# One-hot rows of slot positions: made tile by tile by POOL in place of two halves by DVE

## What is computed

```python
xn = _layernorm(x)
# spiking attention: every projection is normalised and compared with a threshold
Q, K, V = (lif(layer_norm(xn @ W.T + b, g, beta), 1.0) for each of q, k, v)   # zeros and ones
attn = Dh - hamming(Q, K) + log_pe_bias(N, N)       # 16 heads of 16
out = lif(einsum(attn * scale, V), 0.5)
s = lif(layer_norm(out @ Wo.T + bo, go, betao), 1.0)
# feed-forward with 8 experts: each token goes to the nearest centroid
xr = _rms_norm(xn, scale)
ids = argmin(_dist2(xr, centroids))
a, g = split(xr @ up_w[ids]); y = (a * silu(g)) @ down_w[ids]
return x + s * _silu(y + xn)
```

## Time and profile before

| | us |
|---|---|
| median of 3 runs | 417.1 (416.22 to 418.41) |
| the profiled execution's own time | 416.2 |
| its span, first to last instruction | 414.4 |

### The profile page before, as it was taken

One profiled execution on the slowest core, in us unless ns is written; L12 is line 12 of the kernel. 1 busy time (PEld: TensorE's weight loads), 2 busy tenths in 40 slices (PEclk: granted clock), 3 DMA queues, 4 the chain that ended last, 5 costly groups with the idle time before them and its releaser, 6 DMA issues.

```text
span 414.4 us, 10171 instructions
## 1 busy us (share of the span) xinstructions
PE 377.2 (91%) x2661; PEld 315.4 (76%) x2662; DVE 323.3 (78%) x829; ACT 227.6 (55%) x606; POOL 225.3 (54%) x330
## 2 busy tenths in 40 slices
PE   3686999999996889899899999999999999999991
PEld 3665877877785678778678888888888888888881
DVE  4965788898866998987857777787778777778873
ACT  1464778788777033353545555555555555555551
POOL 1245678778773011225744666666666666666642
PEclk9978999999998999999989999999999999999998
DMA  5458466695652021222841222222323223232000
GB/s 192 153 153 254 143 191 177 190 291 149 162 153 76 2 78 30 76 88 68 249 148 43 85 85 67 70 84 86 97 60 93 82 80 89 87 93 67 26 15 0
DMA packets 31649, 44.86 MB, mean 108 GB/s; under 512 B 4041, under 2 KB 25714, under 8 KB 31492
## 3 DMA queue, kind: packets, MB, share of 16 engines
q1 hardware_dynamic: 25040, 29.38, 23.9%
q0 software_dynamic: 6240, 14.71, 12.2%
q10 hardware_dynamic: 340, 0.42, 0.3%
HBM read 36.28 MB, written 15.61 MB: 125 GB/s over the span
## 4 chain that ended last, share of the span: by engine, by line
PE 36%; DMA 19%; DVE 16%; issue 10%; POOL 9%; ACT 5%; POOLq 2%; DVEq 1%; SPq 1%; ACTq 0%
PE bank L556 10%; DMA row_a<-rows_a,slot_id 10%; PE bank L574 10%; DMA xs<-in_x 7%; PE bank L399 4%; ACT d_hi L734 3%; PE bank L445 3%; DMA rows_a<-xn 3%; DVE d_lo L1077 2%; PE bank L528 2%; POOL sq L1165 2%; DVE e_hl L1080 2%; POOL inv_std L1140 2%; DVE up_lo L1035 2%; PE bank L539 2%
## 5 line engine op out<-in xcount | busy, mean ns | idle before, releaser
L1077 DVE TENSOR_TENSOR d_lo<-down_sb,d_hi 128x1024 fp32r<-128x1024 f32 x39 | 47.8, 1225 | 34.2 <-ACT d_hi L734 34.2
L1202 POOL DMA_INDIRECT row_a<-rows_a,slot_id x39 | 41.2, 1057 | 47.1 <-DVE e_o L1091 46.1
L734 ACT ACTIVATE d_hi<-down_sb 128x1024 fp32r x39 | 41.4, 1061 | 45.0 <-PE bank L574 38.8
L1235 POOL DMA_INDIRECT out_x<-e_o,slot_id x39 | 44.0, 1129 | 20.8 <-issue 14.5
L556 PE MATMUL bank<-up_hi,e_xh 128*128 x156 | 52.4, 417 | 0.7 <-ACT e_xh L716 0.7
L556 PE MATMUL bank<-up_hi,e_xl 128*128 x156 | 49.2, 397 | 1.2 <-DVE e_xl L1055 1.2
L556 PE MATMUL bank<-up_lo,e_xh 128*128 x156 | 48.9, 395 | 0.0
L1208 POOL DMA_INDIRECT row_s<-rows_s,slot_id x39 | 39.6, 1017 | 15.8 <-issue 11.6
L399 PE MATMUL bank<-w_hi,x_hi 128*128 128x264 f32 (+1 forms) x128 | 42.5, 414 | 0.8 <-DVE dots L883 0.8
L662 ACT ACTIVATE junk<-bank 128x256 bf16<-128x256 f32 x96 | 36.0, 379 | 9.5 <-PE bank L403 8.4
L685 ACT ACTIVATE junk<-bank 128x256 bf16<-128x256 f32 x32 | 12.0, 383 | 46.9 <-PE bank L479 46.9
(11 more groups left out here) (209 smaller groups left out, 1021.7 us busy)
## 6 DMA issues: line engine op xcount, KB each, us to landing
up_raw<-in_up_w SPq DMA_DIRECT2D x16, 512.0 KB, 5.1
rows_a<-xn SPq DMA_DIRECT2D x32, 128.5 KB, 2.8
xs<-in_x SPq DMA_DIRECT2D x8, 512.0 KB, 3.6
rows_a<-in_x SPq DMA_DIRECT2D x8, 512.0 KB, 6.4
down_sb<-in_down_w SPq DMA_DIRECT2D x8, 512.0 KB, 5.1
rows_s<-s_out SPq DMA_DIRECT2D x8, 256.0 KB, 2.5
blk_tab<-in_blocks SPq DMA_DIRECT2D x1, 1024.0 KB, 5.7
row_a<-rows_a,slot_id POOLq DMA_INDIRECT x39, 3.4
```

The source lines that it names most:

```text
L734: act.activation(d_hi[:, :, :], down_sb[:, bass.ds(e, 1), :, :].rearrange("p a c n -> p (a c) n"), ACT.Copy).then_inc(d_high, 1)
L1077: V.tensor_tensor(d_lo[:, :, :], down_sb[:, bass.ds(e, 1), :, :].rearrange("p a c n -> p (a c) n"), d_hi[:, :, :].bitcast(F32), ALU.subtra ...
L1202: G.indirect_dma_start(row_a[s % 4][:, :], None, rows_a, bass.IndirectOffsetOnAxis(ap=slot_id[:, s:s + 1], axis=0), bounds_check=N - 1, oo ...
L1235: G.indirect_dma_start(out, bass.IndirectOffsetOnAxis(ap=slot_id[:, s:s + 1], axis=0), e_o[s % 4][:, :], None, bounds_check=N - 1, oob_is_ ...
```

## The change

`low_hot` is no longer made by DVE. POOL makes it with one `tensor_scalar` per tile, 16 in each half: the row of column numbers `col_no` (128x128, f32) is compared with one column of `rt[:, 1]` as a scalar per partition. The 16 for q = 0 stand behind `norms_out(0)`, the 16 for q = 1 behind `norms_out(1)`. DVE raises a new semaphore `low_made` behind the instruction that writes `rt[:, 1]`; POOL waits for it ahead of `norms_out(0)`, as it does now for the other conditions of the buffers. POOL raises `low_hots` behind each half, and PE waits for it, besides for `slot_hot`, ahead of the 16 matmuls of that half.

```diff
             for q in range(2):
                 pe.wait_ge(slot_hot, q + 1)
+                pe.wait_ge(low_hots, q + 1)
                 for n in range(HT):
                     last = pe.matmul(bank[6][:, 0:2 * ST], low_hot[q][:, n, :],
...
             step(V.scalar_tensor_tensor(rt[:, 1, :], rt[:, 0, :], -float(P), rt[:, 2, :], ALU.mult, ALU.add))
+            dve.sem_inc(low_made, 1)
...
-                if q == 0:
-                    dve.wait_ge(xt_done, NT)
-                    for k in range(4):
-                        dve.wait_ge(row_put[k], 16 * NT // 4)
-                V.tensor_tensor(low_hot[q][:, :, :], over_s(col_no[:, :], P), per_t(rt[:, 1, ts], P), ALU.is_equal)
                 step(V.tensor_tensor(high_hot[:, :, :], over_s(tile_no[:, :], ST), per_t(rt[:, 0, ts], ST), ALU.is_equal))
...
+            def low_one_hots(q):
+
+                for n in range(HT):
+                    last = G.tensor_scalar(low_hot[q][:, n, :], col_no[:, :], rt[:, 1, q * HT + n:q * HT + n + 1], None,
+                                           ALU.is_equal)
+                last.then_inc(low_hots, 1)
+
+            pool.wait_ge(low_made, 1)
+            pool.wait_ge(tables_made, 6)
+            pool.wait_ge(xt_done, NT)
+            for k in range(4):
+                pool.wait_ge(row_put[k], 16 * NT // 4)
             for c in range(NCH):
                 norms_out(c % 2, c // 2)
+                if c < 2:
+                    low_one_hots(c)
```

More of the change, by code:

```diff
@@ L244, in build @@
             sem("hot_done"), sem("ranks_done"), sem("pos_done"), sem("slot_hot"), sem("slots_summed"), sem("slots_made"))
+        low_made, low_hots = sem("low_made"), sem("low_hots")
         m_done, cvec_done, sv_done = sem("m_done"), sem("cvec_done"), sem("sv_done")
```

## The result

The changed kernel takes 426.6 us (median of 4 runs, 423.2 to 428.4) against 417.4 of the kernel before in the same rounds: a ratio of 1.023, with a 95% interval of 1.018 to 1.028. Timed again twice, it gave 1.026 (1.021 to 1.032) and 1.028 (1.024 to 1.033). By the medians of the three comparisons it is 9 to 11 us slower, where 2.1 were forecast and 5.9 were the end of the range. Now and then an execution of one and the same kernel takes over 1.5% longer than its fastest one: the ratios in this document leave such executions out, the medians and spans hold them, unless one is named as left out.

What follows compares the result with a forecast made beforehand. Bound: a chain of waits through all engines, lastly DVE, to PE's `attend(4)`. POOL's sixteen comparisons (5.3 us per half), holds of 2.0 and 4.5 and 0.13 for the semaphore make `attend(4)` 2.1 us late: 417.1 + 2.1 = 419.2 us, range 415.9 to 423.0.

Steps and rivals of the forecast that it cites:

- The saving on DVE: Ahead of `attend(4)`: removing DVE's second 2.2 us `low_hot` gives PE back its idle 1.27 us and no more.
- the second half makes PE wait: Last 16 slot matmuls wait for POOL's rows, ready at 170.6; `attend(4)` starts at 171.3 instead of 169.21, +2.1 us.
- `a_sp` isn't late any more: On DVE, chunk 3: without the second `low_hot`, `a_sp` moves from 168.43 to 166.2.
- 0.13 us, as forecast: One semaphore raise behind DVE's write of `rt[:, 1]`, on the chain to PE's chunk 2: +0.13 us.
- The prediction's own sign of being wrong: The whole is wrong if POOL's last `low_hot` came before 166.6, or a price above 0.38 us moved chunk 1's norms.
- the price of one POOL instruction: One 128-column POOL comparison, start to start: 0.33 us, between ends 0.21 and 0.45; sixteen are 5.3 us.
- the upper end of 0.45: Price of one POOL comparison bounded above by a two-input tensor_tensor: 0.45 us, 7.2 for sixteen, `attend(4)` +6.0 us.
- The holds: POOL stands still while DVE runs instructions with two SBUF inputs: 2.0 us in the first gap, 4.5 in the second.
- The norms of chunk 1: On POOL behind the first sixteen comparisons: reached at 158.6 where due at 158.54, 0.1 us late.
- POOL's power: Two columns take 0.70 us; a comparison done in that manner would cost tens of us, chance 4 in 100.
- mutual hindrance: POOL's comparison far dearer than the two-input row, or DVE and POOL hindering each other more; chance 0.06.
- the dear case: Comparison at 0.38 us or more overruns POOL's 7.21 us gap: +3.7 us at 0.38, +6.0 at 0.45; chance 0.17.

Runs made afterwards that it cites:

- the measuring list: Kernel before, plus POOL instructions that only measure, behind its last scatter; a 128-column tensor_scalar took 0.58 us from start to start, the span says nothing.
- The experiment with the first half alone: Against the kernel before, only tiles 0 to 15 of `low_hot` go to POOL, DVE makes the rest at its old place; 423.5 us, ratio 1.016.

## Why the prediction was wrong

**What it had right.** The saving on DVE is bounded by PE's idle 1.27 us; the question is whether POOL's work fits in its gaps; the second half makes PE wait in the place of the wait removed; `a_sp` isn't late any more; from 5.2 us for sixteen on, the first half holds up the norms of chunk 1 and each us counts twice. The raise of `low_made` makes the step behind that instruction 0.16 us instead of 0.04, and PE's wait ahead of `attend(2)` 1.28 instead of 1.15: 0.13 us, as forecast. The prediction's own sign of being wrong, a price above 0.38 us that moves the norms of chunk 1, is what came.

**The step that failed is the price of one POOL instruction**, "I take the middle, 0.33 us". It is 0.58. The middle was wrong, and so was the upper end of 0.45: it took a row with two inputs as a bound for a form with one. The only tensor_scalar in the trace had two columns, which says nothing of the price by the column: 2.5 ns, against the 2.14 that I worked out for two inputs. The subtraction with a broadcast column takes 0.36, less than the bound, so the two forms differ in the other direction than I assumed. With 0.58, sixteen are 9.3 us instead of 5.3.

**The holds were mis-sized the other way.** Forecast 2.0 and 4.5 us, measured 1.1 and 2.2 (10.4 and 11.5 us for what takes 9.3 alone). I added up the whole of DVE's instructions, less 0.07 us each. As the measuring list shows, some 0.45 of a POOL instruction of 0.58 runs beside DVE's next one. In the changed kernel the held ones take 0.93 to 1.32 us at `high_hot` and `high_id` and 1.33 at `up_lo`, where 1.1 and more were forecast. Had I had the right price with these holds, the sum would have come to +10 us ahead of `attend(4)` instead of the 7.2 measured; the two errors have opposite signs, and the first is the larger.

**The norms of chunk 1** were 3.0 us late instead of 0.1, which follows from the price: 9.3 + 1.1 against a gap of 7.2. The experiment with the first half alone shows it by itself, +2.5 us at `attend(4)`.

**A term that was missing.** The idle time of PE itself was priced as time lost, and not what it does to the granted clock. The trace of the kernel before had it on view in small: a wait of 2.3 us ahead of 131.9, and behind it a grant near the lower level from 132 to 134 us (the row has the clock third from its end):

```profile
131.89 0.27 PE L411 MATMUL bank<-ident,q_sp 128*128 128x128 bf16 x2 [2.32 <-DVE q_t L889]
132.00:134.00 2.00, 1.48 (x15) 1.19 (x14) 1.28 (x4) 1.22 (x2) 0.00 (x0) 0.57 0.00 0
```

In the changed kernel the term is 1.2 to 2.3 us: 0.8 to 1.9 behind `attend(4)` and 0.4 ahead of it.

**The range** ended at 423.0 because the upper end of the price was a two-input row. The measured price lies beyond that row and far short of POOL's power, the only dearer case that was priced; for all of this the prediction had 0.06, together with more mutual hindrance. The way of the dear case, the first half late and each us counted twice, was the one that came.

## What to carry to other kernels

An instruction that moves to another engine has the price of its own form there, and a row of another form is no bound for it, even if it reads more: where the trace has none, the range must reach well past the nearest row, or the form be measured first in a list behind the kernel's end. A gap of an engine is as long as the other engine lets it be: eight comparisons that POOL does in 4.6 us alone took 5.8 to 8.05 us in its gaps, by what DVE did beside them. And before work is moved off an engine that is late at one place, look whether it idles elsewhere: two low parts put into DVE's idle time gave 1.9 us, where the move could have given 1.1 at best.

## What the runs showed of the hardware

- POOL tensor_scalar: 0.25 us and 2.5 ns for each column, the same for comparison and multiplication, for a column and a constant as scalar, and for bf16 and f32 output; tensor_tensor with a broadcast second input 0.36 us and cast 0.24 us at 128 columns, all from start to start.
- Beside back-to-back DVE instructions with two SBUF inputs (1.23 to 1.28 us each) POOL gets one of its 0.58 us instructions for each, 1.31 us apart; beside PSUM inputs it loses nothing (9.30 us for 16). DVE pays too: two `up_lo` take 2.72 us instead of 2.48.
- A PE wait of 8 us was followed by matmuls at 1.2 GHz (28 matmuls in 2.5 to 3.2 us instead of 1.74) until the grant rose; with 34 useless matmuls in the wait the grant stayed at 1.00.
- On DVE sixteen tensor_scalar of 128 f32 columns take 3.2 us, one tensor_tensor of 2048 2.2 us.
